# Layers 2 and 3 attention: a PSUM bank per product, and another cycle of TensorE's work

## What is computed

```python
def _L3_xattn_ref(hidden_states, encoder_hidden_states, Wq, Wk, Wv, Wo, bo):
    q = hidden_states @ Wq
    k = encoder_hidden_states @ Wk
    v = encoder_hidden_states @ Wv
    q = q.reshape(B, S, H, Dh).transpose(0, 2, 1, 3)
    ...
    scores = jnp.einsum('bhsd,bhkd->bhsk', q, k) * scale
    probs = jax.nn.softmax(scores, axis=-1)
    out = jnp.einsum('bhsk,bhkd->bhsd', probs, v)
    out = out.transpose(0, 2, 1, 3).reshape(B, S, H * Dh)
    out = out @ Wo + bo
    return out
...
    x = x + _L2_xattn_ref(_layernorm(x, axis=-1), ctx_768, ...)
    ...
    x = x + _L3_xattn_ref(_layernorm(x, axis=-1), ctx_768, ...)
```

## Time and profile before

| | us |
|---|---|
| runs without the profiler | 1447.54, 1449.80, 1448.45; median 1448.45 |
| span of the profiled execution | 1450.7 |
| TensorE busy in the span | 1374.7 (95%) |
| VectorE, ScalarE, GpSimd busy | 1000.6, 945.3, 743.7 |
| layer 2 attention, 522 to 776 us | 254, of it TensorE busy 246.6 |
| layer 3 attention, 918 to 1417 us | 499, of it TensorE busy 491.7 |

### The profile page before, as it was taken

The page is one execution under the profiler, slowest core; times in us unless marked ns, Lnnn a source line. Parts: engine busy times, 40 slices in busy tenths (PEclk is TensorE's granted clock), DMA queues, the critical chain, the costliest instruction groups (busy, mean ns, idle before and its releaser), DMA issues. The chain is left out here.

```text
span 1450.7 us, 30070 instructions
## 1 busy us (share of the span) xinstructions
PE 1374.7 (95%) x9799; PEld 1008.5 (70%) x9799; DVE 1000.6 (69%) x2375; ACT 945.3 (65%) x1951; POOL 743.7 (51%) x763
## 2 busy tenths in 40 slices
PE   7999989998998989999998998999999999999998
PEld 5555548897665867777775777677777777777766
DVE  6877846677657667777776566576767767677683
ACT  4787776775666556666664465576766667676663
POOL 5455641111752146666655576465656556565642
PEclk9999999999999999999999999899999999999999
DMA  6300000000001300000001000000000000000002
GB/s 172 82 0 0 1 15 16 1 1 1 1 1 48 88 0 2 2 0 0 0 0 37 1 0 2 0 1 1 1 0 0 0 0 0 0 0 0 1 6 83
DMA packets 31517, 20.57 MB, mean 14 GB/s; under 512 B 9569, under 2 KB 29000, under 8 KB 31432
## 3 DMA queue, kind: packets, MB, share of 16 engines
q1 hardware_dynamic: 31204, 19.38, 4.8%
q10 hardware_dynamic: 228, 0.10, 0.0%
HBM read 18.42 MB, written 1.05 MB: 13 GB/s over the span
## 5 line engine op out<-in xcount | busy, mean ns | idle before, releaser
L2354 POOL TENSOR_TENSOR arena<-arena,l3a_rinv 128x512 f32<-128x512 f32 x256 | 258.9, 1040 | 205.8 <-DVE l3a_rinv L2735 205.4
L2631 ACT ACTIVATE arena<-l3a_scores_ps,l3a_nmax 128x512 f32<-128x512 f32 x256 | 174.7, 685 | 118.5 <-DVE l3a_nmax L2729 118.5
L2354 POOL TENSOR_TENSOR arena<-arena,l2a_rinv 128x512 f32<-128x512 f32 x128 | 129.4, 1040 | 96.1 <-DVE l2a_rinv L2735 95.2
L2729 DVE TENSOR_REDUCE l3a_nmax<-l3a_scores_ps 128x2 f32<-128x1024 f32 x128 | 156.0, 1219 | 19.5 <-PE l3a_scores_ps L2427 19.4
L874 ACT ACTIVATE l0a_prob<-l0a_scores_ps,l0a_k_scale 128x1024 f32<-128x1024 f32 x128 | 135.5, 1112 | 35.2 <-PE l0a_scores_ps L724 34.5
L2440 PE MATMUL l3a_turned_ps<-const,arena 128*128 128x128 f32 x1024 | 144.7, 274 | 3.0 <-DVE l3a_probT L2741 1.6
L2741 DVE COPY l3a_probT<-l3a_turned_ps 128x512 f32<-128x512 f32 x128 | 88.5, 691 | 80.6 <-PE l3a_turned_ps L2440 80.4
L2440 PEld LDWEIGHTS l3a_turned_ps<-const,arena 128*128 128x128 f32 x1024 | 119.3, 141 | 26.1 <-issue 8.5
L2451 PE MATMUL l3a_work_ps<-l3a_probT,l3a_v 128*64 128x256 f32 x1024 | 125.3, 387 | 2.3 <-DVE x_tokens L2756 1.6
L2631 ACT ACTIVATE arena<-l2a_scores_ps,l2a_nmax 128x512 f32<-128x512 f32 x128 | 87.4, 686 | 56.4 <-DVE l2a_nmax L2729 56.4
L2451 PEld LDWEIGHTS l3a_work_ps<-l3a_probT,l3a_v 128*64 128x64 f32 x1024 | 69.4, 137 | 52.8 <-issue 24.0
(11 more groups left out here) (768 smaller groups left out, 3609.4 us busy)
## 6 DMA issues: line engine op xcount, KB each, us to landing
l1f_w<-in_L_ffn_w SPq DMA_DIRECT2D x16, 256.0 KB, 2.7
arena<-in_ctx SPq DMA_DIRECT2D x4, 384.0 KB, 5.4
w_l_w<-in_L_ffn_W SPq DMA_DIRECT2D x1, 1024.0 KB
arena<-in_L_ffn_W SPq DMA_DIRECT2D x16, 64.0 KB, 1.8
out_x<-x_tokens SPq DMA_DIRECT2D x8, 128.0 KB, 1.9
x_tokens<-in_x SPq DMA_DIRECT2D x1, 896.0 KB, 7.5
const<-in_constants SPq DMA_DIRECT2D x1, 525.0 KB
w_l_wo<-in_L_xattn_Wo SPq DMA_DIRECT2D x1, 512.0 KB
```

The source lines that it names most:

```text
L2354: e.tensor_tensor(prob[n][:, :], prob[n][:, :], bcast(rinv[:, n:n + 1], [P, S]), ALU.mult).then_inc(m.prob_ready, 1)
L2631: e.activation(prob[at][:, :], bank(u), ACT.Exp, bias=nmax[:, at:at + 1], accum_out=rsum[:, at:at + 1]).then_inc(m.exp_ready, 1)
L2729: e.tensor_reduce(nmax[:, at:at + 2], sps[:, i * 1024:(i + 1) * 1024].rearrange("p (h k) -> p h k", h=2), AX.X, ALU.max, negate=True).then ...
```

## The change

Six things change together.

1. The turned units get a bank each. T0 and T1 go into the two banks whose scores of pair n have been exponentiated (`turned_bank`: u < 2), T2 into `work[1]`, T3 into `tps[0]`.
2. The scores of odd turns take the four banks in the order 2, 3, 0, 1 (`place`). So the first half of S waits for all exponentials of the turn before, the second for the copies of T0 and T1.
3. Q, J, the turned tokens and the small products go into `tps[1]`; W and V share `work[0]`; K and T2 share `work[1]`.
4. TensorE's order in a turn is S, (J), W, (tokens), T0, T1, T2, T3, V, Q, K.
5. The waits follow the banks: K waits for `k_low` and for VectorE's copy of T2, V for `keep_o`, W for the copy of V; Q in turn c = 2 waits for the update of x.
6. ScalarE's order is exponentials 0, 1, 2, copy of T1, exponential 3, copy of T3, copy of V, q, k. VectorE's order stays; it reads other banks.

The core of the diff:

```diff
+        def place(b, c, u):
+            return u if c % 2 == 0 or (is_first(b) and c == 1) else (u + 2) % UNITS
+        def scores_bank(b, c, u):
+            return bank(place(b, c, u))
+        def turned_bank(b, c, u):
+            return scores_bank(b, c, u) if u < 2 else (work[1], tps[0])[u - 2]
...
             def project_k(b, c, side):
-                if isinstance(n, int) and n < AHEAD:
-                    wait(e, m.k_lo_ready, n)
-                else:
-                    e.wait_ge(m.v_kept, n + 1)
+                wait(e, m.k_lo_ready, n)
+                if not isinstance(n, int) or n > AHEAD:
+                    e.wait_ge(m.pT_kept_dve, 2 * n - 4)
...
             def scores(b, c, halves=range(TPB)):
-                    wait(e, m.exp_ready, UNITS * (n - 1) + 2 * i + 2)
+                    if is_first(b) and c == 1:
+                        e.wait_ge(m.exp_ready, 2 * i + 2)
+                    elif i == (0 if is_first(b) and c == 2 else 1):
+                        wait(e, m.pT_kept_dve, 2 * n - 3)
+                        wait(e, m.pT_kept_act, 2 * n - 3)
+                    else:
+                        wait(e, m.exp_ready, UNITS * n)
...
+            def turned_in_cycle(b, c, turn_c, more, u):
+                n = C * b + c
+                if u < 2:
+                    e.wait_ge(m.exp_ready, UNITS * n + u + 1)
+                elif u == 2:
+                    e.wait_ge(m.k_lo_ready, n + 2 if c + 1 < C or more else C * B)
+                elif is_first(b) and c == 1:
+                    e.wait_ge(m.v_kept, 2)
+                turned(*turn_c, u, turned_bank(b, c, u))
...
             def turn(b, side, more):      # TensorE
-                        e.wait_ge(m.x_updated, TPB * b)
-                        weighted(*back)
-                        project_v(*on)
-                        turned(*turn_c, 0)
-                        project_q(*on)
-                        turned(*turn_c, 1)
-                        project_k(*on)
-                        turned(*turn_c, 2)
-                        turned(*turn_c, 3)
+                    weighted(*back, n + 2 if c + 1 < C or more else C * B)
+                    turned_in_cycle(b, c, turn_c, more, 0)
+                    turned_in_cycle(b, c, turn_c, more, 1)
+                    turned_in_cycle(b, c, turn_c, more, 2)
+                    turned_in_cycle(b, c, turn_c, more, 3)
+                        e.wait_ge(m.o_kept, n - 1)
+                        project_v(*on)
+                        if c == 2 and not first:
+                            e.wait_ge(m.x_updated, TPB * b)
+                        if c == 3:
+                            e.wait_ge(late.z_lo_ready, 1) if first else e.wait_ge(ahead.z_kept, b)
+                        project_q(*on)
+                        project_k(*on)
...
             def turn(b, side, more):      # ScalarE
                     exps(b, c, 2)
+                    keep_turned(*turn_c, 1, turned_bank(b, c, 1))
+                    exps(b, c, 3)
+                    keep_turned(*turn_c, 3, turned_bank(b, c, 3))
                     if onward:
                         keep_v(*on)
-                    exps(b, c, 3)
-                        keep_turned(*turn_c, 1)
                         keep_q(*on[0:2])
                         keep_k(*on[0:2])
-                        keep_turned(*turn_c, 3)
```

More of the change, by code:

```diff
@@ L2291, in out_bank @@
         def out_bank(b):
-            return (tps[1], bank(1), bank(0))[b % 3]
+            return (work[1], bank(1), bank(0))[b % 3]
         def turns(e, turn):
@@ L2385, in project_q @@
                 wait(e, m.q_lo_ready, n)
[L2386 to L2389, removed]
+                e.matmul(tps[1][:, 0:T], wq_hi[:, pair], z_hi[:, tokens], start=True, stop=False)
+                e.matmul(tps[1][:, 0:T], wq_lo[:, pair], z_hi[:, tokens], start=False, stop=False)
+                e.matmul(tps[1][:, 0:T], wq_hi[:, pair], z_lo[:, tokens], start=False, stop=True).then_inc(m.q_projected, 1)
             def project_k(b, c, side):
@@ L2404, in project_v @@
             def project_v(b, c, side, out=None):
-                n = C * b + c
-                out = work[1] if out is None else out
+                out = work[0] if out is None else out
                 half = slice(c // KT * 512, (c // KT + 1) * 512)
                 keys = slice(c % KT * P, (c % KT + 1) * P)
-                if not isinstance(n, int) or n >= AHEAD:
-                    e.wait_ge(m.k_lo_ready, n)
                 if c == 0:
@@ L2487, in turn @@
                     turn_c = (b, c - 1) if c >= 1 else (b - 1, C - 1)
[L2488 to L2493, removed]
+                    choosing = experts and not more
+                    if c == 0 and first:
                         scores(b, c)
-                    if c == 0 and first:
                         project_q(0, 1, 0)
                         project_k(0, 1, 0)
-                        project_v(0, 0, 0, tps[0])
+                        project_v(0, 0, 0)
                         keep_warm(8)
@@ L2514, in turn @@
                     if c == 2 and not first:
-                        e.wait_ge(m.q_lo_ready, n + 2)
-                        for i in range(TPB):
-                            last = join(b - 1, i, work[0][:, i * P:(i + 1) * P], range(C))
-                        last.then_inc(m.y_ready, 1)
-                        if onward:
-                            project_v(*on)
-                        e.wait_ge(m.x_updated, TPB * b)
-                    if c >= 2 or not first:
-                        if c + 1 < C or more:
-                            e.wait_ge(m.q_lo_ready, n + 2)
-                        weighted(*back)
@@ new lines, in turn @@
+                        for i in range(TPB):
+                            last = join(b - 1, i, tps[1][:, i * P:(i + 1) * P], range(C))
+                        last.then_inc(m.y_ready, 1)
+                    weighted(*back, n + 2 if c + 1 < C or more else C * B)
+                    if c == 3:
+                        if onward:
+                            turn_finished(b - 1, n - 1)
+                        else:
+                            e.wait_ge(m.q_lo_ready, C * B)
+                            ahead.tensor(e, b - 1, tps[1])
@@ L2792, in turn @@
                         invert(b, c, 0)
-                        update(b - 1, [work[0][:, i * P:(i + 1) * P] for i in range(TPB)])
+                        update(b - 1, [tps[1][:, i * P:(i + 1) * P] for i in range(TPB)])
                         ahead_statistics(b - 1)
@@ L2833, in _ @@
             keep_o(B - 1, C - 2)
[L2834 to L2835 removed]
+            keep_turned(B - 1, C - 1, 0, last_turned_bank(0))
+            keep_turned(B - 1, C - 1, 2, last_turned_bank(2))
             keep_o(B - 1, C - 1)
[L2837 removed]
+            update(B - 1, [tps[1][:, 0:D], bank(0)[:, 0:D]])
             if experts:
```

164 lines of the change are left out of this document (80 added, 84 removed).

## The result

The changed kernel takes 1497.88 us (median of 4 runs, 1493.41 to 1499.2). The kernel before, timed beside it, takes 1449.12 us (1447.54 to 1449.91). The ratio is 1.033, with a 95% interval of 1.0307 to 1.0352: **slower by 3.3%**, or 48.8 us. The forecast was 1491 us, with a range of 1474 to 1502; the time lies 6.9 us over the forecast, inside the range. The profiled execution after has a span of 1496.9 us, to be set against the 1450.7 us of the earlier trace rows.

The account below looks back on a forecast made before the run. TensorE was taken as the bound, with K's new wait for the copy of T2 lengthening each turn: +38.3, +7.2, -2.2, -0.5 and -0.7 make +42.1 us on 1448.45, 1490.6, say 1491 us; range 1474 to 1502.

Parts of the forecast that it names:

- What bounds the kernel: Whole kernel: TensorE busy 95% of 1450.7 us, ScalarE and VectorE not far behind; the ordinary attention turn decides the result.
- The loop and its links: Ordinary turns: S, maxima, exponential 2, copy of T1, exponential 3, reciprocal, copy of T2, K, S; 7.20 to 7.86 us.
- The two estimated distances: In an ordinary turn: reciprocal to copy of T2 taken as 0.14 us, copy's end to K as 0.12 us.
- TensorE's own turn: Attention turns if nothing else waited: 7.15 us, ends 7.1 and 7.2, worth -3.5 us over 71 turns.
- Turns c = 3 and c = 2: Attention turns with extra work: c = 3 at 8.05 us, +0.55 each; c = 2 -0.1 in layer 3, -0.25 in layer 2.
- The waits that go: TensorE's waits of W for x and of T0 for the late tokens vanish: at most 7.4 us together.
- the first rival: K's wait for the copy of T2 doesn't decide; the turn is TensorE's own: -3.5 and -7.4, about 1437 us; chance 0.07.
- the count of 58 ordinary turns: Turns of both attentions with K behind T, counted alike: 58 x 0.66 = +38.3 us.
- T1 late too: Second rival: T1 slips by 0.3 us waiting for its bank, 0.1 a turn, 7 us more: 1498; chance 0.12.
- The clock: TensorE's granted clock in the attentions: expected at 1.00; a lower one was the third rival, over 1502 us, chance 0.07.
- The third rival: TensorE's clock at 0.91 throughout because of pauses, 0.2 us a turn: 1491 + 14 = 1505 us; chance 0.07.
- the place that I had read as 0.91: 11 us stretch of the kernel before with the densest waits, TensorE busy 8.55 us, granted clock 0.91.

Follow-up runs that it names:

- the first experiment: Changed kernel with VectorE's copy of T2 moved ahead of the second reciprocal in every turn: 1428.86 us, ratio 0.9863.
- the fifth experiment: Changed kernel with the copy of T2 ahead of the second reciprocal, plus W again waiting for the update of x in turns c = 2: 1445.61 us, ratio 0.9982.
- The fourth experiment: Changed kernel with the router's small VectorE operations behind the copy of T2, only in turns 4 and 5 of layer 3's last batch: 1491.21 us, ratio 1.0287.
- its repetition: Second set of runs of the changed kernel with the copy of T2 ahead of the second reciprocal: 1431.15 us, ratio 0.9879.

## Why the prediction was right, and where it was off

**What bounds the kernel.** The reading that an ordinary turn decides, and that TensorE is the bound with the others close behind, held. The account above puts 48.9 us on the two attentions.

**The loop and its links.** Shown. An ordinary turn was forecast at 7.86 and is 7.84 to 7.87 in the loops; in the batches that are written out it is 7.70 to 7.75 (7.16 before). There the reciprocal stands at 5.97, the copy follows it by 0.08 us and not by 0.16, and K starts 0.15 behind the copy's end and not 0.06. The links: copy of T1 to exponential 3 0.48, as read before; exponential 3 to reciprocal 0.81; reciprocal to copy 0.16 to 0.17, where I took 0.14 between 0.1 and 0.17; copy's end to K 0.06, where I took 0.12; K to S 0.89, where I took 0.90. The two estimated distances missed by +0.03 and -0.06 and cancelled in part, which was luck. The 0.15 us from copy to restart that I had read in the earlier trace rows stood in a written-out batch, and there the changed kernel has it again. TensorE alone would have had K at about 6.3; freed, it has it at 6.37.

**TensorE's own turn.** I had 7.15, with ends 7.1 and 7.2; the first experiment shows 7.12.

**Turns c = 3 and c = 2.** Turns c = 3 were forecast at 8.05 and are 8.08 to 8.11 in the loops (+0.60 where I had +0.55). In layer 3 the turn c = 2 kept its 11.48, where I had -0.1; in layer 2 it lost 0.19, where I had 0.25.

**The waits that go.** They went. I said at most 7.4 us, and this term is mis-sized for the case that K is free: the first experiment's attentions are 17.1 us shorter than before (237.9 and 481.5, S to S, against 245.8 and 490.7), where the first rival had 3.5 + 7.4 = 10.9. Turns c = 2 fell by 0.60 and 0.78 us in the two layers, while the rows read 0.27 and 0.5: I had left out the wait of Q for the bank that it shared with W, some 0.3 us in each of 13 turns (the fifth experiment's section has the rows). Turns c = 3 fell from 7.5 to 7.37, and five of the six turns that end a pass of layer 3's loop from 7.33 to 7.38 to 7.11; the cause of these is open. The rival's price was 1437; the kernel that meets its condition takes 1429 to 1431.

**Where 6.9 us came from.** Some 2.6 us of it is in the measure and not in the kernel: the medians differ by 48.8 us, the spans of the two profiled executions by 46.2. Between the spans 4.1 us more than the forecast 42.1 are left. The step that failed is the count of 58 ordinary turns, into which I put c = 4 and c = 5 of layer 3's last batch. In the kernel before they took 7.43 and 8.63 us, so with +0.66 each I had 8.09 and 9.29; they took 9.48 and 13.32, which is 5.4 us more. I had laid out VectorE's program between the reciprocal and the copy from an ordinary turn, where nothing stands between them. The fourth experiment gives back 6.7 us. The rest is of both signs and comes to -1.3 us: the first four turns of layer 2 +1.1, and that varies between executions (their first was 6.04 us in the first experiment and 7.27 in its repetition, with the same program); turns c = 2 and c = 3 together +1.3; the ordinary turns that are written out or end a pass of the loop -1.5, as I had counted them like the others; what lies behind the last S -2.9, where I had -0.7. That the total came so near is therefore in part luck.

**T1 late too.** Did not happen: the copy of T1 stands at 4.75, as laid out.

**The clock.** Not in the ordinary turns, with their pause of 0.5 to 0.6 us in each; in the last batch, where the pauses are longer, yes. Windows of the changed kernel, with the columns of the earlier trace rows: a stretch of the loop first, then the last batch from the pause of 1.86 us on, which ends at 1435.96.

```profile
1140.00:1200.00 60.00, 56.41 (x410) 41.33 (x408) 40.04 (x76) 37.92 (x95) 33.77 (x36) 1.00 0.00 0
```

```profile
1434.20:1437.40 3.20, 1.44 (x9) 0.98 (x11) 1.88 (x4) 1.00 (x3) 1.69 (x2) 1.00 0.00 0
1437.40:1441.90 4.50, 4.50 (x27) 2.37 (x23) 2.96 (x3) 2.35 (x7) 0.00 (x0) 0.62 0.01 2
...
1448.60:1452.00 3.40, 3.40 (x11) 2.30 (x13) 0.35 (x2) 0.60 (x1) 0.00 (x0) 0.50 0.00 0
```

At a mean of 0.62 most of the second of these stretches ran at the lower level, 1.2 GHz. TensorE in this turn:

```profile
1436.82 0.50 PE L2443 MATMUL l3a_scores_ps<-l3a_k_hi,l3a_q_hi 64*128 64x512 f32 x2
...
1439.08 2.86 PE L2473 MATMUL l3a_work_ps<-l3a_probT,l3a_v 128*64 128x256 f32 x16
1441.87 1.09 PE L2451 MATMUL l3a_scores_ps<-const,arena 128*128 128x128 f32 x8
```

S to W is 2.26 us there and 1.59 in the ordinary turn; W to T0 2.79 and 1.88. Together 1.58 us, and VectorE's copy of what W left waited 1.12 us for W, so a part of the 13.32 us is the clock's. The third rival had its mechanism right and its place wrong: the end of the last batch, not all turns. The rule of the Trainium skill that I cited ("TensorE: Matmul & The Clock Gate", section "A second HAM failure mode: psum-queue depth-cycling"), that frequent short pauses make the clock swing, is not borne out by the turns of the loops, which have such a pause each: the clock is 1.00 over layer 2 from 556 to 777 us and over layer 3 from 930 to 1427 us. It agrees with the place that I had read as 0.91. There the kernel before has three pauses of TensorE, 0.42, 0.85 and 0.49 us, close behind each other at a clock of 1.00 (from 1406.0 to 1409.5 us it is busy for 1.74 us), and behind them 2.5 us at 0.61.

## What to carry to other kernels

When a change of buffers hangs the last instruction of an in-order program on another engine's copy, lay out that engine's own queue in front of the copy: what it waits for there is waited for by the whole turn. A copy that frees a bank goes ahead of an operation that has to wait for something later, as long as its own input is ready; here those two lines were worth 67 to 69 us, and turned a loss of 3.3% into a gain of 1.2 to 1.4%. And count turns by what stands in them, batch by batch: the batch with other work in it was the one mis-sized most.

## What the runs showed of the hardware

**The lower clock came behind pauses of TensorE, but the length of a pause alone does not say when.** Pauses of 0.5 us in every turn left it at 1.00, and one of 0.97 us in each turn c = 2 of the fifth experiment left the transposes after it at 1.09 us for eight, as in any turn. In the kernel before two waits of 1.2 us for the late tokens, at 551 and 947 us, were followed by 1.00 as well, and so was the one of 1.09 us that ended at 1400.09. After 1.86 us the clock stayed at 1.00 for some 1.4 us and was then 0.62 for 4.5 us; after 1.68 us in the fourth experiment's last batch it came to 0.53 for 2.75 us, after 1.50 us in the first experiment's to 0.50 for 3.0 us, and after 3.71 us it was 0.50 for 3.4 us. But the 0.61 above came behind three pauses of 0.85 us at most. No run changed the pauses alone.

**Tiny operations of VectorE can take a microsecond.** The router's 7 x 8 operations took 0.21 us in some places and 0.9 to 1.1 us in others. VectorE's rows beside those shown above, and GpSimd's of the same time:

```profile
1442.45 0.21 DVE L2112 TENSOR_SCALAR l3a_early_w<-const,l3a_early_red 7x8 f32<-7x8 f32 x1
1442.69 0.93 DVE L2113 TENSOR_SCALAR l3a_early_w<-l3a_early_w 7x8 f32<-7x8 f32 x1
1443.65 0.96 DVE L2114 TENSOR_TENSOR l3a_early_w<-l3a_early_w 7x8 f32<-7x8 f32 x1
```

```profile
1442.56 2.04 POOL L2368 TENSOR_TENSOR arena<-arena,l3a_rinv 128x512 f32<-128x512 f32 x2 [6.67 <-DVE l3a_rinv L2760]
1445.49 2.04 POOL L2368 TENSOR_TENSOR arena<-arena,l3a_rinv 128x512 f32<-128x512 f32 x2 [0.89 <-DVE l3a_rinv L2760]
```

Two merged products start at 1445.49, each about 1.02 us; they end near 1446.51 and 1447.53. VectorE's two operations end at 1446.55 and 1447.55. The same holds at 1442.56: products that end near 1443.58 and 1444.60, operations that end at 1443.62 and 1444.61; the one that took 0.21 us had begun before GpSimd did. So each lasted until the GpSimd product beside it was done. In the turn before, a reduction of the same 7 x 8 tile ran while GpSimd had four products, which went on from 1431.86 to 1435.90, and took 0.15 us:

```profile
1434.01 0.90 DVE L2095 TENSOR_TENSOR l3a_early_w<-l3a_early_w,const 7x8 f32<-7x8 f32 x1
1434.94 0.15 DVE L2096 TENSOR_REDUCE l3a_early_red<-l3a_early_w 7x1 f32<-7x8 f32 x1
```

In the kernel before the same operations took 0.93 and 0.95 us (lines 2113 and 2114), so it is no effect of the change. The Trainium skill, "SBUF — State Buffer", section "Who interferes with whom", says that a VectorE instruction with two SBUF inputs, or in a mode that uses both ports, and a GpSimd instruction exclude each other for a whole instruction, and that a reduction is not touched; the trace agrees in all of these rows. I made no run that separates it from other causes.
